# Head attention and feed-forward as one stage over token tiles, in plain fp32, with two norms joined

## The chip, the core and the metric

The kernel runs on one core of one Trainium2 chip. A core has five engines with queues of their own that run side by side: TensorE (matmuls, PE in the profile; its weight loads are PEld), VectorE (DVE), ScalarE (ACT), GpSimd (POOL) and SyncE (SP, which here issues transfers). The metric is the device time of one execution, in microseconds.

## What is computed

A three-part model layer on x of 8 x 64 tokens by 512. First cross attention over a context of 1601 rows. Then the part that is edited, and last a mixture of experts with routing. The edited part, cut from the reference (the outer call applies a norm without gain to x, and the part begins with a norm of its own):

```
x = x + xattn(layernorm(x), ctx)                 # cross attention; its last product is W_O
y = layernorm(x)                                 # no gain, no bias
h = layernorm(y) * ln1_g + ln1_b                 # the second norm in a row
q, k = per-token 32 heads of 16 from h @ Wq.T, h @ Wk.T;  v = h @ Wv.T
att = softmax(nan_to_num(q @ k.T))               # 32 x 32 for each token, heads attend to heads
att2 = att[first half, first half] - lam * att[second half, second half]
o = rmsnorm(att2 @ v) * (1 - 0.8 + 0.6 exp(-0.3))
conn = y + o @ Wo.T + bo
src3 = relu((layernorm(conn) * ln2_g + ln2_b) @ W1.T + b1) @ W2.T + b2     # 512 -> 2048 -> 512
x = x + conn + src3
```

## The kernel before

The 512 tokens are four tiles of 128 (`TT`), tokens on partitions, 512 features along them; a feature-major copy of a tile is four blocks of 128 (`KD`). Stages follow one another, each a block with its own queues and an all-engine barrier behind it: `queries`, `cross_attention`, `head_attention`, `feed_forward`, `route`, `experts`. The order of an engine's work is written out by hand, and semaphores link the engines.

In `head_attention` and `feed_forward` every matmul is done as three (`mm3`, L64 to L66): both operands are split into a high and a low part of type fp32r (ScalarE copies the high part, `high`; GpSimd subtracts to get the low one, `low`, L790), and high x high, high x low, low x high are added. In order: `W_O` is applied to the output of cross attention for all four tiles, x and the bias (added beforehand by GpSimd, L838) are added on VectorE (L997), `normaliser` runs twice over all tiles (`norm1`, `norm2`, L658 to L670), TensorE turns the result, ScalarE applies gain and bias, VectorE splits (L1002, L1004), and 12 projections (three a tile) follow.

The attention of heads has no matmul, since each token has its own 32 x 32 scores. `order` lists products: for each tile `NQ` = 8 pieces "qk" of `QR` = 4 query heads (2048 elements a partition) and `NA` = 4 pieces "av"; the av pieces of a tile come behind the qk pieces of the next. Of three pieces GpSimd multiplies two into the buffers of `prod` (three) and VectorE one into `vprod` (two) (`multiply`, L761 and L765); VectorE reduces all of them (`reduce`, L943). Between them stand `clean` (nan_to_num: L950, L951, and the sum on GpSimd, L807), `row_max` (L955, L957), 32 exponentials a tile on ScalarE with the bias from `nmax` (L906), `row_sum` (L961, and `rlam`, L963), `weights` on GpSimd (L814 to L821), `square`, `mean_square`, `root`, `scale` (L827 to L974). Then TensorE turns the tile (L1077) and applies `Wo`, and `skip` adds it (L984). `low(4)`, for `Wo`, stands in GpSimd's queue among the products of tile 1.

`feed_forward` loads eight more slabs of weights through three buffers, normalises and turns all tiles, and runs 16 steps: `up(f)` makes 128 hidden features for all 512 tokens, ScalarE applies relu (L1177), VectorE and GpSimd split (L1193, L1150), `down(f)` adds to all four tiles.

## Time and profile before

| | us |
|---|---|
| median of 3 runs | 1822.5 (1821.58 to 1823.15) |
| the profiled execution, its own time | 1819.43 |
| its span, first to last instruction | 1817.6 |
| mean granted TensorE clock | 0.887 |
| VectorE busy | 958.4 (53%) |
| TensorE busy | 1425.5 (78%) |
| GpSimd busy | 654.7 (36%) |

How rows are read. A row of the span's slices has 40 digits, one for each 45.4 us: the busy share in tenths, and for PEclk the granted clock in tenths of 2.4 GHz. A row of stretches gives from:to, its length, then for PE, PEld, DVE, ACT and POOL the busy time with the number of instructions, the granted clock, the share of the DMA engines and GB/s. A row of instruction groups gives line, engine, operation, out<-in by name, shape out<-in, count, then busy time in us and mean ns of one, and the idle time before them with what ended it. A row of the timeline gives start, length (of the whole row where it stands for several instructions), engine, line, and in brackets the idle time before it. A plain fp32 matmul has two records.

### The profile page before, as it was taken

What the parts mean: (1) busy time and instruction counts of PE and PEld (TensorE: products, weight loads), DVE (VectorE), ACT (ScalarE), POOL (GpSimd) and SP (SyncE); (2) the same over time, 40 slices, a digit from 0 to 9 for tenths busy, and PEclk for the clock granted to TensorE, in tenths of its full rate; (3) what the DMA queues carried; (4) which work ended last, traced back from release to release, by engine and by line L of the source; (5) the groups of instructions that cost most, each with busy time, mean ns of one, the idle gap of its engine ahead of it and who ended that gap; (6) DMA issues with size and microseconds to landing.
All of it is one profiled execution on the core that took longest, in us unless ns stands there. A gap on an engine that the chain in (4) does not pass through costs nothing. (4 is left out here: it accounts for less than half of the span.)

```text
span 1817.6 us, 23549 instructions
## 1 busy us (share of the span) xinstructions
PE 1425.5 (78%) x8688; PEld 1217.8 (67%) x8688; DVE 958.4 (53%) x2159; ACT 612.2 (34%) x1230; POOL 654.7 (36%) x260
## 2 busy tenths in 40 slices
PE   3599999999999999999996630112389565999995
PEld 2599999999999999999995420001267453555552
DVE  7155545555555555555554598995601553444443
ACT  4144344443445434454434232112321201232231
POOL 4505023050220502205003599895652312344442
PEclk8799999999999999999998765555689686999997
DMA  3401002010020200201003000000500209999999
GB/s 140 167 7 61 25 1 79 7 62 24 1 79 7 79 7 1 80 7 43 1 1 117 35 0 0 0 1 0 191 1 0 99 1 361 336 333 337 342 331 304
DMA packets 42619, 166.70 MB, mean 92 GB/s; under 512 B 5792, under 2 KB 6304, under 8 KB 33952
## 3 DMA queue, kind: packets, MB, share of 16 engines
q1 hardware_dynamic: 32352, 141.32, 21.2%
q0 software_dynamic: 10176, 24.12, 5.3%
q8 instruction: 62, 1.02, 0.2%
q14 instruction: 29, 0.24, 0.0%
HBM read 144.98 MB, written 20.45 MB: 91 GB/s over the span
## 5 line engine op out<-in xcount | busy, mean ns | idle before, releaser
L331 POOL TENSOR_TENSOR c_hi<-craw,ones 128x1608 fp32r<-128x1608 f32 x32 | 91.9, 2871 | 621.8 <-PE ps_x L66 548.1
L64 PE MATMUL ps_x<-wkv_hi,c_hi 128*128 128x256 f32 (+1 forms) x832 | 240.3, 289 | 0.0
L65 PE MATMUL ps_x<-wkv_lo,c_hi 128*128 128x256 f32 (+1 forms) x832 | 233.4, 281 | 0.0
L66 PE MATMUL ps_x<-wkv_hi,c_lo 128*128 128x256 f32 (+1 forms) x832 | 232.8, 280 | 0.0
L64 PE MATMUL ps_x<-c_hi,wkv_hi 128*128 128x402 f32 x512 | 196.2, 383 | 34.0 <-POOL c_lo L334 34.0
L583 DVE TENSOR_TENSOR pT<-ps_x,pT 128x512 fp32r<-128x512 f32 (+1 forms) x224 | 145.6, 651 | 125.9 <-ACT pT L508 122.7
L65 PE MATMUL ps_x<-c_lo,wkv_hi 128*128 128x402 f32 x512 | 178.0, 348 | 0.0
L66 PE MATMUL ps_x<-c_hi,wkv_lo 128*128 128x402 f32 x512 | 177.5, 347 | 0.0
L508 ACT CAST pT<-ps_x 128x512 fp32r<-128x512 f32 (+1 forms) x224 | 124.6, 557 | 140.2 <-PE ps_x L418 136.6
L553 DVE TENSOR_TENSOR vv<-ps_x,vv 128x512 fp32r<-128x512 f32 (+1 forms) x112 | 73.0, 652 | 176.7 <-ACT vv L489 176.7
L64 PEld LDWEIGHTS ps_x<-wkv_hi,c_hi 128*128 128x128 f32 (+1 forms) x832 | 153.2, 184 | 16.9 <-issue 16.9
L489 ACT CAST vv<-ps_x 128x512 fp32r<-128x512 f32 (+1 forms) x112 | 62.3, 556 | 288.1 <-PE ps_x L66 288.1
L1772 PE MATMUL ps_e<-e_w_gu,e_xT 128*128 128x512 f32 x344 | 157.5, 601 | 0.0
L547 DVE SCALAR_TENSOR_TENSOR kT_lo<-ps_x,bk,kT_hi 128x402 fp32r<-128x402 f32 x128 | 81.4, 636 | 140.8 <-ACT kT_hi L483 140.8
L65 PEld LDWEIGHTS ps_x<-wkv_lo,c_hi 128*128 128x128 f32 (+1 forms) x832 | 153.5, 184 | 0.0
L66 PEld LDWEIGHTS ps_x<-wkv_hi,c_lo 128*128 128x128 f32 (+1 forms) x832 | 153.3, 184 | 0.0
L1077 PE MATMUL ps_h<-ident,h_on 128*128 128x128 f32 x16 | 4.4, 432 | 178.8 <-POOL h_on L833 178.8
L433 PE MATMUL ps_x<-pT,vv 128*128 128x256 f32 (+1 forms) x832 | 135.1, 285 | 2.5 <-DVE pT L583 2.5
L566 DVE TENSOR_SCALAR_CACHE_REDUCE prob<-ps_x 128x402 f32<-128x402 f32 (+1 forms) x256 | 131.2, 569 | 0.0
L433 PEld LDWEIGHTS ps_x<-pT,vv 128*128 128x128 f32 (+1 forms) x832 | 124.8, 188 | 5.3 <-DVE pT L583 3.9
L418 PE MATMUL ps_x<-ident,prob 128*128 128x128 f32 (+1 forms) x832 | 127.0, 272 | 0.0
L1077 PEld LDWEIGHTS ps_h<-ident,h_on 128*128 128x128 f32 x16 | 2.9, 217 | 180.8 <-issue 99.0
(290 smaller groups left out, 3232.2 us busy)
## 6 DMA issues: line engine op xcount, KB each, us to landing
e_w_gu<-w_gu SPq DMA_DIRECT2D x49, 1024.0 KB, 8.1
craw<-ctxT SPq DMA_DIRECT2D x32, 804.0 KB, 4.5
e_w_dn<-w_dn SPq DMA_DIRECT2D x48, 512.0 KB, 5.6
f_raw<-slabs SPq DMA_DIRECT2D x8, 1024.0 KB, 4.8
h_raw<-slabs SPq DMA_DIRECT2D x5, 1024.0 KB, 4.9
qbd_dram<-qbd_all SPq DMA_DIRECT2D x2, 2048.0 KB, 6.9
qbd<-qbd_dram SPq DMA_DIRECT2D x16, 256.0 KB, 2.7
wraw<-w_qkv SPq DMA_DIRECT2D x3, 1024.0 KB, 8.4
```

The lines of the kernel that those rows point to most:

```text
L64: nc.tensor.matmul(out, a_hi, b_hi, start=start, stop=False)
L65: nc.tensor.matmul(out, a_hi, b_lo, start=False, stop=False)
L66: return nc.tensor.matmul(out, a_lo, b_hi, start=False, stop=stop)
L331: nc.gpsimd.tensor_tensor(c_hi[:, :, chunk(c)], craw[:, c % 2], ones[:, 0:1].unsqueeze(2).to_broadcast([P, KD, CW]), ALU.mult).then_inc(sp ...
L418: ins = nc.tensor.transpose(ps[0:r, 6 + n % 2, c:c + P], prob[:, 2 * g + j, P * st:P * st + r], ident[:])
L433: ins = nc.tensor.matmul(ps[:, 4 + g, 256 * j:256 * j + 256], vv[0:r, st, 2 * g + j].rearrange("p l c -> p (l c)"), pT[0:r, n % 2, st % 2, ...
L508: nc.scalar.copy(pT[0:r, n % 2, 0:w, :, 0].rearrange("p a j c -> p (a j) c"), ps[0:r, 6 + n % 2, 0:256 * w].rearrange("p (a c) -> p a c", ...
L547: nc.vector.scalar_tensor_tensor(kT_lo[:, m, chunk(c)], ps[:, n % KEY_BANKS, 0:CW], bk[:, 2 * h + m:2 * h + m + 1], f32(kT_hi[:, m, chunk( ...
L553: nc.vector.tensor_tensor(vv[0:r, 2 * v:2 * v + w, :, 1].rearrange("p a j c -> p (a j) c"), ps[0:r, V_BANK[v], 0:256 * w].rearrange("p (a ...
L566: ins = nc.vector.tensor_scalar(prob[:, p, CW * n:CW * n + w], ps[:, 2 * (i % 2) + j, 0:w], 0.0, None, ALU.add, ALU.max, accum_out=pmax[:, ...
L583: nc.vector.tensor_tensor(pT[0:r, n % 2, 0:w, :, 1].rearrange("p a j c -> p (a j) c"), ps[0:r, 6 + n % 2, 0:256 * w].rearrange("p (a c) -> ...
L1772: ins = nc.tensor.matmul(ps[:, GU], xT[:, b, P * g:P * g + P], w_gu[:, b, g], start=(g == 0), stop=(g == KD - 1))
```

## The change

One stage, `head_and_feed_forward`, takes the place of two, and everything from `W_O` on goes tile by tile.

- All 13 weight slabs stay in SBUF as they are (12 buffers; the last slab takes the place of the first). There is no `mm3` in the stage and no high or low part: each matmul is one in plain fp32. Biases come in through a matmul of one row (`ones` by `row`) that opens the sum.
- The two norms in a row use one set of statistics: with v the variance, the second variance is v/(v + eps), and `normed_twice` applies the product of both inverse roots in one pass; `normed_once` gives y. Tiles are normalised in groups 0, 1, and 2 with 3.
- `QR` is 2: twice as many pieces of half the size. The rule of one in three on VectorE stays. `row_max` negates in the reduction, `rlam` moves to ScalarE, z2 is written in place.
- q, k and v have two buffers. Feed-forward of a tile is `up` with 128 columns (tokens) moving, relu on ScalarE, and `down` six steps behind, with eight buffers `fT` (`NF_`); its PSUM is two banks of four pieces each.
- Work of all three kinds is put by hand into the queues, in ScalarE's and TensorE's as below.

```diff
-    NR, NS, NP, NPV = 2, 3, 3, 2
-    QR = 4
+    NP, NPV = 3, 2
+    QR = 2
+    FT, NF_, LAG = FF // P, 8, 6
@@ reductions on VectorE, what stands among them
-                    if t >= 2 and i == 2:
-                        mean_square(t - 2)
-                    if t and i == 4:
-                        row_sum(t - 1)
+                    if t == 0 and i == 3:
+                        attended_in(2)
+                    if t == 0 and i == 5:
+                        attended_in(3)
+                        first_norm(2)
+                    if t == 0 and i == 8:
+                        inverse(2)
...
+                    if t == 0 and i in (10, 12):
+                        normed_twice(2 if i == 10 else 3)
+                        normed_once(2 if i == 10 else 3)
+                    if t >= 2 and i == 3:
+                        mean_square(t - 2)
                     if t >= 2 and i == 5:
                         root(t - 2)
-                    if t >= 2 and i == 7:
-                        attended_low(t - 2)
+                    if t and i == 6:
+                        row_sum(t - 1)
+                    if t >= 3 and i == 9:
+                        second_skip(t - 3)
+                    if t >= 2 and i == 12:
+                        connect(t - 2)
+                        second_norm(t - 2)
+                    if t >= 2 and i == 14:
+                        connection_normed(t - 2)
@@ VectorE behind the last reduction
+            second_skip(TT - 3)
+            connect(TT - 2)
+            second_norm(TT - 2)
             mean_square(TT - 1)
+            connection_normed(TT - 2)
             root(TT - 1)
+            connect(TT - 1)
+            second_norm(TT - 1)
+            second_skip(TT - 2)
+            connection_normed(TT - 1)
+            second_skip(TT - 1)
@@ ScalarE
+            act.wait_ge(c_loaded, 64)
+            std_first(0)
+            turned_h(0)
+            query_key(0)
+            std_first(1)
+            value(0)
+            turned_h(1)
+            query_key(1)
+            value(1)
+            std_first(2)
...
+            turned_c(0)
+            hidden(0, range(0, 4))
+            exponentials(2, range(0, 16))
+            hidden(0, range(4, 8))
+            exponentials(2, range(16, 32))
+            root(1)
+            scaled_sums(2)
+            hidden(0, range(8, 16))
+            value(3)
+            turned_o(1)
+            std_second(1)
+            turned_c(1)
+            hidden(1, range(0, 4))
+            exponentials(3, range(0, 16))
+            hidden(1, range(4, 8))
+            exponentials(3, range(16, 32))
+            scaled_sums(3)
+            root(2)
+            hidden(1, range(8, 16))
...
@@ TensorE
-                    ins = mm3(nc, ps[:, 4 + f % 4], w_hi[s % NS][:, g, c], w_lo[s % NS][:, g, c], a_hi[:, g], a_lo[:, g],
-                              g == 0, g == KD - 1)
+                    ins = nc.tensor.matmul(ps[:, UP + f // 4 % 2, c], slab[:, 5 + 2 * (f // 4), g, c], cT[:, g],
+                                           start=(g == 0), stop=(g == KD - 1))
...
+            attend(0)
+            attend(1)
+            turn_h(0)
+            for w in range(3):
+                project(0, w)
+            attend(2)
+            attend(3)
...
+            turn_h(3)
+            turn_o(0)
+            put_out(0)
+            project(3, 0)
+            project(3, 1)
+            turn_c(0)
+            for f in range(FT + LAG):
+                if f < FT:
+                    up(0, f)
+                if f >= LAG:
+                    down(0, f - LAG)
+            project(3, 2)
+            turn_o(1)
+            put_out(1)
+            turn_c(1)
...
+            for f in range(FT + LAG):
+                if f < FT:
+                    up(2, f)
+                if f >= LAG:
+                    down(2, f - LAG)
+                if f == 9:
+                    turn_o(3)
+                if f == 13:
+                    put_out(3)
+            turn_c(3)
```

The new functions called there: `attend(t)` is bias row and four matmuls with `W_O`; `attended_in(t)` adds x; `first_norm` and `inverse` make the joined norm's factors, with `std_first` on ScalarE between; `turn_h`, `turned_h`, `project`, `query_key`, `value` make q, k, v; `turn_o`, `turned_o`, `put_out` apply `Wo`, and `connect` adds it to y; `second_norm`, `std_second`, `connection_normed`, `turn_c`, `turned_c` make the input of the feed-forward; `second_skip(t)` waits for `down_full` of the whole tile t and adds it to x, to which GpSimd's `skip(t)` has added conn. `hidden(t, fs)` is relu of some of the 16 pieces; a piece needs its batch of four ups, and the `down` eight pieces back for its buffer. `up` waits at every fourth piece for relu of the batch before, and `down(t, f)` for relu of piece f.

## Rows read from the trace of the kernel before

**Rows 1.** The page's slices, 40 of 45.4 us each

```profile
DVE  7155545555555555555554598995601553444443
PEclk8799999999999999999998765555689686999997
```

**Rows 2.** Busy time by stretch, around the edited stages

```profile
976.20:1032.50 56.30, 27.37 (x94) 21.28 (x95) 25.80 (x48) 18.23 (x19) 27.32 (x6) 0.67 0.33 122
1032.50:1258.80 226.30, 40.01 (x151) 30.41 (x149) 195.52 (x101) 60.93 (x278) 200.93 (x55) 0.58 0.00 0
1258.80:1275.60 16.80, 10.43 (x28) 7.50 (x28) 3.80 (x8) 0.80 (x2) 2.09 (x2) 0.67 0.00 0
1275.60:1409.80 134.20, 98.92 (x400) 78.47 (x400) 40.21 (x42) 28.83 (x29) 66.63 (x26) 0.85 0.18 65
1409.80:1523.00 113.20, 60.71 (x265) 50.74 (x266) 59.12 (x159) 12.68 (x15) 24.75 (x13) 0.68 0.32 118
```

**Rows 3.** The timeline at the stage's opening and the first products

```profile
981.14 1.90 ACT L874 CAST h_w_hi<-h_raw 128x2048 fp32r<-128x2048 f32 x1 [2.36 <-DMA h_raw<-slabs]
987.66 0.79 PE L64 MATMUL ps_h<-h_w_hi,h_a_hi 128*128 128x512 f32 x1 [13.37 <-POOL h_w_lo L790]
988.49 3.69 DVE L991 TENSOR_TENSOR h_lprod<-h_lam 128x32 f32<-128x32 f32 x1 [8.78 <-DMA h_lam<-lambdas]
1028.53 1.11 ACT L894 ACTIVATE h_q<-ps_h 128x512 f32<-128x512 f32 x1 [6.43 <-PE ps_h L66]
1032.51 31.55 POOL L761 TENSOR_TENSOR h_prod<-h_q,h_k 128x2048 f32<-128x2048 f32 x6 [13.20 <-ACT h_k L894]
```

**Rows 4.** Groups of instructions by shape, 980 to 1500 us

```profile
L761 POOL TENSOR_TENSOR h_prod<-h_q,h_k 128x2048 f32<-128x2048 f32 x21 | 108.5, 5198 | 13.2 <-ACT h_k L894 13.2
L943 DVE TENSOR_REDUCE h_att<-h_prod 128x128 f32<-128x2048 f32 x21 | 47.7, 2279 | 21.7 <-POOL h_prod L761 21.7
L906 ACT ACTIVATE h_ex<-h_att,h_nmax 128x32 f32<-128x32 f32 x128 | 39.0, 306 | 71.0 <-DVE h_nmax L957 71.0
L807 POOL TENSOR_TENSOR h_att<-h_z 128x1024 f32<-128x1024 f32 x4 | 9.4, 2353 | 7.8 <-DVE h_z L951 7.8
L955 DVE TENSOR_REDUCE h_rmax<-h_att 128x32 f32<-128x1024 f32 x4 | 4.8, 1212 | 2.4 <-POOL h_att L807 2.4
L984 DVE TENSOR_TENSOR oT<-ps_h,oT 128x512 f32<-128x512 f32 x4 | 2.7, 686 | 9.5 <-PE ps_h L66 9.5
L670 DVE TENSOR_SCALAR h_hT<-oT,h_n_mv,h_n_rstd 128x512 f32<-128x512 f32 x4 | 1.9, 541 | 0.0
L814 POOL TENSOR_TENSOR h_w<-h_ex,h_rinv 128x256 f32<-128x256 f32 x4 | 2.5, 618 | 2.9 <-DVE h_rlam L963 2.8
L827 POOL TENSOR_TENSOR h_sq<-h_o 128x512 f32<-128x512 f32 x4 | 6.2, 1554 | 8.3 <-DVE h_o L943 8.3
```

**Rows 5.** Timeline of weight loads: experts' 512-column matmul, cross attention's 128-column one

```profile
1600.37 0.19 PEld L1787 LDWEIGHTS ps_e<-e_w_dn,e_hT 128*128 128x128 f32 x1 [0.24 <-issue]
1600.80 0.19 PEld L1787 LDWEIGHTS ps_e<-e_w_dn,e_hT 128*128 128x128 f32 x1 [0.24 <-issue]
...
805.13 0.53 PEld L403 LDWEIGHTS ps_x<-diag,ones 128*128 128x128 f32 x4
805.57 0.19 PEld L64 LDWEIGHTS ps_x<-c_hi,wkv_hi 128*128 128x128 f32 x1
```

**Rows 6.** Busy time by stretch, in the feed-forward, behind a pause of TensorE

```profile
1323.50:1327.90 4.40, 4.32 (x10) 3.47 (x11) 0.00 (x0) 0.00 (x0) 2.41 (x2) 0.50 0.00 0
1327.90:1345.00 17.10, 17.10 (x74) 13.73 (x73) 1.99 (x3) 3.87 (x4) 7.55 (x4) 0.99 0.01 1
```

**Rows 7.** Timeline: GpSimd's products, and one small VectorE instruction twice

```profile
1070.12 26.33 POOL L761 TENSOR_TENSOR h_prod<-h_q,h_k 128x2048 f32<-128x2048 f32 x5
1092.52 3.96 DVE L963 TENSOR_SCALAR h_rlam<-h_rinv,h_lam 128x16 f32<-128x16 f32 x1
1152.15 0.23 DVE L963 TENSOR_SCALAR h_rlam<-h_rinv,h_lam 128x16 f32<-128x16 f32 x1
```

More of the change, by code:

```diff
@@ new lines, in attend, with turn_h @@
+            def attend(t):
+                out = ps[:, WIDE if t % 2 == 0 else DOWN]
+                if t >= 2:
+                    pe.wait_ge(x1_done, t - 1)
+                nc.tensor.matmul(out, ones[0:1, :], row[0:1, 0], start=True, stop=False)
+                for g in range(KD):
+                    ins = nc.tensor.matmul(out, oT[:, g, P * t:P * t + P], slab[:, W_O, g], start=False, stop=(g == KD - 1))
+                ins.then_inc(x1_full, 1)
+            def turn_h(t):
+                pe.wait_ge(h_done, t + 1)
+                if t:
+                    pe.wait_ge(hT_done, t)
+                for g in range(KD):
+                    ins = nc.tensor.transpose(ps[:, TURN, P * g:P * g + P], h[:, t % 2, P * g:P * g + P], ident[:])
+                ins.then_inc(hT_full, 1)
@@ new lines, in project @@
+            def project(t, w):
+                pe.wait_ge(hT_done, t + 1)
+                pe.wait_ge(w_loaded[W_Q + w], 16)
+                if t:
+                    if w < 2:
+                        pe.wait_ge(qk_done, 2 * (t - 1) + w + 1)
+                    else:
+                        pe.wait_ge(v_done, t)
+                for g in range(KD):
+                    ins = nc.tensor.matmul(ps[:, QKV + w], hT[:, t % 2, g], slab[:, W_Q + w, g], start=(g == 0), stop=(g == KD - 1))
+                ins.then_inc(qkv_full, 1)
@@ new lines, in turn_o, with put_out @@
+            def turn_o(t):
+                pe.wait_ge(on_done, t + 1)
+                if t == 0:
+                    pe.wait_ge(hT_done, TT)
+                else:
+                    pe.wait_ge(cT_done, t)
+                    pe.wait_ge(onT_done, t)
+                for g in range(KD):
+                    ins = nc.tensor.transpose(ps[:, TURN, P * g:P * g + P], on[:, P * g:P * g + P], ident[:])
+                ins.then_inc(onT_full, 1)
+            def put_out(t):
+                pe.wait_ge(onT_done, t + 1)
+                pe.wait_ge(w_loaded[W_OUT], 16)
+                if t == 0:
+                    pe.wait_ge(x1_done, TT)
+                else:
+                    pe.wait_ge(conn_done, t)
+                nc.tensor.matmul(ps[:, WIDE], ones[0:1, :], row[0:1, 1], start=True, stop=False)
+                for g in range(KD):
+                    ins = nc.tensor.matmul(ps[:, WIDE], onT[:, g], slab[:, W_OUT, g], start=False, stop=(g == KD - 1))
+                ins.then_inc(src_full, 1)
@@ L1232, in _, with down @@
-            for f in range(FT + 2):
-                if f < FT:
-                    up(f)
-                if f >= 2:
-                    down(f - 2)
+            def down(t, f):
+                n = FT * t + f
+                if f == 0:
+                    if t == 0:
+                        pe.wait_ge(x1_done, TT)
+                    else:
+                        pe.wait_ge(x2_done, t)
+                    nc.tensor.matmul(ps[:, DOWN], ones[0:1, :], row[0:1, 2], start=True, stop=False)
+                if t == 0 and f % 4 == 0:
+                    pe.wait_ge(w_loaded[6 + 2 * (f // 4)], 16)
+                pe.wait_ge(f_done, n + 1)
+                nc.tensor.matmul(ps[:, DOWN], fT[:, n % NF_], slab[:, (6 + 2 * (f // 4)) % LATE, f % 4], start=False, stop=(f == FT - 1)
+                                 ).then_inc(down_full, 1)
```

632 lines of the change are left out of this document (307 added, 325 removed).

## The prediction

> **What bounds the kernel now.** I read the share of the span first [rows 1], then the busy time of each engine in stretches around the edited code [rows 2], then the order of time at its two ends [rows 3], and last the groups of instructions by shape for prices [rows 4]. The first thing to see is that the edited stage is one piece of the span with nothing beside it: it opens behind an all-engine barrier at 976.2 us and its last vector add ends at 1409.8 us, 433.6 us out of 1817.6. Route and experts follow behind barriers and are untouched, as is cross attention, so every microsecond taken from the stage comes off the end, and nothing else can give or take. Inside it there are four stretches with different limits. From 976.2 to 1032.5 is a serial opening (56.3 us): load, split weights, project, two norms one after the other, turn, project. From 1032.5 to 1258.8 VectorE and GpSimd are the bound, 195.5 and 200.9 us busy of 226.3, and TensorE works 40 us of it, mostly the tail of the projections. From 1258.8 to 1275.6 (16.8 us) the last tile's output projection is waited for. From 1275.6 to 1409.8 (134.2 us) the feed-forward runs alone, TensorE 98.9 us busy, the others mostly idle. TensorE idle in one long stretch and vector engines idle in the next: that is what a pipeline over tiles can use [rows 2].
>
> **Prices of a plain fp32 matmul.** No matmul of this stage is plain fp32 today, but the experts have 512-column ones: each is two records, and two weight loads of the stream start 0.43 us apart (1600.37, 1600.80), so one matmul costs 0.86 us at full clock [rows 5]. A 128-column one (ones by diag) is two records too, and four records take 0.44 us (805.13 to 805.57): 0.22 us each [rows 5]. A split product's single matmul of 512 columns takes 17.1 / 74 = 0.231 us in the warm stretch of the feed-forward [rows 6], so the three of `mm3` cost 0.69 us. Dropping the splits therefore raises TensorE's time by a quarter (0.86 against 0.69). The Trainium skill speaks against the change here too: "FP8 and Floating Point Precision", section TensorE Precision Notes, says that true FP32 takes 4 passes through the array, against three for the split; by that rule the ratio would be 4/3 where the rows give 1.24, so the trace agrees in direction and the rows' figure is smaller.
>
> **The opening.** Removed: the copies to high parts, the GpSimd low parts and with them the wait until 987.66; the second pass of norm statistics; the splits of the turned tile; and the opening now needs tile 0 only. New path: slab 0 has landed at 981.1 (ScalarE starts on it at 981.14, TensorE only at 987.66 [rows 3]). TensorE is at half clock then, a matmul costs 2 x 0.86; five per tile (bias row and four), at half clock for 5 to 6 us (4.4 in [rows 6]; here it has stood still longer), so tile 0 is ready at about 988.3 and tile 1 at 992.6. Tile 0's add and joined norm take about 2.5 us on VectorE, to 990.8; but ScalarE first waits for all four small loads, queued behind 4 MB now. In the profile the lambdas behind 3.5 MB were there at 988.5 [rows 3]; half a MB more and two more loads put that at about 992. Then root, inverse, one normalising pass (0.54 us, [rows 4]) to 993.3, four transposes and four evictions to 995.2, two projections of 4 x 0.86 us and the eviction of q and k (1.1 us each, [rows 3]) to 1003.6. The first product starts there and not at 1032.5: **28.9 us saved**. The other tiles' start-up work goes beside the products; inverse of tiles 2 and 3 waits on ScalarE, which comes to it only behind both projected tiles at about 1027, some 4 us after VectorE: I count 2 us, since GpSimd fills its three buffers meanwhile.
>
> **The loop of products.** QR goes from 4 to 2: 96 products of 1024 elements for 48 of 2048, still one in three on VectorE. Two engines share something: GpSimd's run of five products takes 26.33 us and the small VectorE instruction issued beside it at 1092.52 takes 3.96 us, until GpSimd's product ends at 1096.45, where a like one takes 0.2 us alone [rows 7]; a reduction keeps its 2.28 us beside GpSimd [rows 4]. So I add up, over the loop, GpSimd's time and that of VectorE's two-input and scalar instructions, and leave the reductions out. (The Trainium skill, "SBUF — State Buffer", section Who interferes with whom, calls it an exclusive lock that is held for the whole instruction and never taken by `tensor_reduce`. By that rule the two times add up as well, and the trace agrees.) Before: 32 products x 4.45 us free of waits (an estimate: 26.33 less two VectorE products of about 2.3, over 5, and less a little), `low(4)` 4.5, per tile the sum 2.3 and three weights of 0.6 to 0.7, 17.6 in all, squares and scales 6.3 (six of about 1.0 free of waits, 1.55 with them [rows 4]), and on VectorE 16 x 2.3 + 7.6: 214.7 us against 226.3 measured, so 11.6 us did not overlap. After: 64 products x 2.28 (half of 4.45 and some 0.05; a 1024-element add takes 2.35, [rows 4]) = 146, sums, weights, squares, scales 23.9, two skips 2.5, no `low(4)`; VectorE 32 x 1.2 + 5.2 + normalising passes and small ones 5.6 = 49.2. Sum 221.6; with smaller pieces I take 9.4 us of lost overlap instead of 11.6: 231 us, **4.7 us dearer**. VectorE's own list stays below it: 96 reductions at 1.14 (1.21 alone, [rows 4]) 109, products 54 with waits, the new norm work about 20, less the fused negation and the scaled sums moved to ScalarE (about 15).
>
> **The waits that the pipeline adds.** VectorE's queue holds `second_skip(0)` behind the tenth product of tile 3, and behind it stand all later reductions, for which GpSimd's three buffers wait. It needs all of feed-forward tile 0. ScalarE's order lets `hidden(0, 8..16)` run only behind `root(1)` and `scaled_sums(2)`, that is, behind VectorE's `row_sum(2)` at the seventh product of tile 3. By then TensorE has come to down(8), which waits for it; behind it are one up and eight downs in all: 4 x 0.22 + 8 x 0.86 = 7.8 us at full clock, about 10.8 because it stood still before and starts at half clock [rows 6]. VectorE arrives three products (6 us) after `row_sum(2)`: a wait of 4.8 us. `connect(1)` then needs project(3, 2) 3.4, turn and two ScalarE copies 2.1, put_out 4.3 after that, against an add and three products, 6 us: 3.8 us more. Of these 8.6 I count **7 us** lost, since GpSimd runs ahead by its three buffers. Exponentials (9.8 us a tile, 32 x 0.306, [rows 4]) are beside the products as before. The loop: 231 + 2 + 7 = 240 us, so its last reduction is at 1003.6 + 240 = 1243.6, not at 1258.8.
>
> **The tail.** Feed-forward of tiles 0 and 1 has gone beside the products; tiles 2 and 3 have not. What is left of tile 1 behind `root(2)` (10.8 us) and put_out(2) (6) is shorter than the products of av(3) (19), so nothing of it is waited for. Then two adds, statistics, mean_square(3), normalise (add 0.68, pass 0.54, [rows 4]), turn, evict: 5.5 us. Tile 2 on TensorE: 64 x 0.22 + 17 x 0.86 = 28.7 us, plus turn_o(3) and put_out(3) inside it 4.8, plus 2.8 for a start at half clock: 36.3. Then `second_skip(2)` stands ahead of `connection_normed(3)`: 3.5 us until tile 3 is turned. Tile 3: 28.7 + 2.5 for the clock. Last add and clearing of the semaphores 2.6. Together 79.1: the next stage starts at 1322.7 in place of 1410.0.
>
> **Sum.** -28.9 (opening) + 13.7 (loop 240 for 226.3) - 72.1 (16.8 + 134.4 after the loop, now 79.1) = -87.3 us. The profiled execution took 1819.4 us by its own time (span 1817.6), so the changed one should take 1732.1; the median of the timed runs lies 3.1 us above that profiled execution, so I forecast **1735 us**.
>
> **Rivals.** (a) *Half clock in the first two feed-forward tiles.* TensorE stands still in each of them, waiting for ScalarE. At 1.2 GHz tile 0 ends at about 1187, project and put_out bring tile 1's start to 1210, it takes 57 us, put_out(2) ends at 1279 and not before the last reduction: the tail starts 35 us later, **1770 us**. For it: the granted clock was 0.50 for 4.4 us behind a pause. Against: it was 0.99 right after [rows 6]. (b) *The half-size pieces overlap better.* A wait for the other engine's instruction is half as long; if lost overlap falls from 11.6 to 3 us and all stalls to 4, the loop takes 229: **1724 us**. For it: the wait of 3.96 us is that of a whole 2048-element product [rows 7]. Against: the reductions are no shorter in sum. (c) *Slower: TensorE at half clock is the bound of the stage.* Four times 57.4 us from the start of feed-forward tile 0 at 1133, project 7, three put_outs 26, and the hand-overs (turn, evict, norm, 5 us each) 20 are 282: the stage ends at 1416, 6 us later than today, **1828 us**. Each microsecond at full clock gives one back, so it is slower than before only if all but some 6 us of that stretch stay at 1.2 GHz. Against it: 17.1 us of unbroken matmuls at 0.99 [rows 6], and in tiles 2 and 3 fT holds eight pieces, so nothing interrupts TensorE for long. By the Trainium skill, "TensorE: Matmul & The Clock Gate", section HAM oscillation, a stream with recurring pauses drops back to the slow clock each time; that would be (a) in the first two tiles, and [rows 6] shows both levels, not which one the new loop gets.
>
> **How the numbers follow.** Forecast 0.57, (a) 0.18, (b) 0.22, (c) 0.03. Around the forecast, lost overlap (3 to 18 us), the stalls (3 to 15) and the half-clock starts (0 to 6) reach some 10 us down and 15 up: 1725 to 1750 by itself. The range takes in (b) with some of that, and (a): 1714 to 1772; left out are (c) and the outer ends of the others. This kernel can be told from no change at about 0.2%: faster 0.96, same 0.01, slower 0.03.
>
> **What would show it.** First product at 1004 us; 96 reductions at about 1.2 us each; a VectorE wait for TensorE's last `down` of tile 0 in tile 3's products, about 5 us; the last reduction near 1244; granted clock 1.0 in both last feed-forward tiles and 29 us each; the next stage at 1323. Wrong if the first product waits for loads, if GpSimd's half-size product takes clearly more than 2.3 us, or if a 128-column plain matmul doesn't stream at 0.22 us with 128-column weights loaded for each.

## The result

The changed kernel takes **1744.1 us** (median of 4 runs, 1742.1 to 1745.7) against 1822.0 us before (4 runs, 1821.1 to 1823.2): a ratio of 0.957, 95% interval 0.956 to 0.959, or 78 us less. The forecast was 1735 us, range 1714 to 1772. The profiled execution took 1745.7 us (span 1743.8), where the sum had given 1732.1: it is 13.6 us above the sum.

TensorE's slices of before first (VectorE's are in [rows 1]), then the page of after, its share of busy time and its slices:

```profile
PE   3599999999999999999996630112389565999995
```

```profile
PE 1475.6 (85%) x8888; PEld 1213.9 (70%) x8888; DVE 912.6 (52%) x2185; ACT 600.7 (34%) x1297; POOL 559.6 (32%) x263
...
PE   3499999999999999999999762276795668999994
...
DVE  6145455555555555555555399885702733444442
...
PEclk9699999999999999999999886587897677999997
```

A slice is 43.6 us. VectorE's full slices (9988, the 24th to 27th, with the 5 and 7 behind them) now have TensorE at 2 to 7 tenths (622767). Before, the two took turns: VectorE's 9899 (the same places, of 45.4 us each) stand beside TensorE's 3011. The same in stretches cut where the work changes: opening, products, tail, route and experts (to set beside [rows 2]; columns are the length, busy us of each engine, granted clock, DMA share, GB/s):

```profile
977.30:1005.40 28.10, 21.30 (x44) 8.68 (x45) 5.49 (x17) 7.66 (x13) 0.04 (x1) 0.81 0.94 376
1005.40:1253.40 248.00, 134.21 (x484) 75.93 (x482) 207.13 (x191) 77.08 (x338) 197.31 (x88) 0.76 0.04 17
1253.40:1332.10 78.70, 68.19 (x346) 46.80 (x346) 7.61 (x19) 13.11 (x44) 4.57 (x4) 0.93 0.00 1
1332.10:1743.80 411.70, 331.74 (x1200) 196.32 (x1200) 185.71 (x717) 90.42 (x185) 137.07 (x99) 0.87 0.81 270
```

| stretch | before | predicted | after |
|---|---|---|---|
| stage opens | 976.2 | 976.2 | 977.3 |
| opening, to the first product | 56.3 | 27.4 | 28.1 |
| products, to the last reduction | 226.3 | 240 | 248.0 |
| behind the last reduction | 151.2 | 79.1 | 78.7 |
| route, experts, output | 407.5 | 407.5 | 411.7 |

("Before", the stretch behind the last reduction is the 16.8 us and 134.4 us of the prediction.) So opening and tail came as worked out, to 1 us. The miss is 8 us in the products, 4.2 us in code that the change does not touch, and 1.1 us by which the stage opens later. The opening and the first steps of the products, on VectorE, ScalarE and GpSimd of after (to set beside [rows 3]):

```profile
991.97 0.21 DVE L1070 TENSOR_SCALAR h_var<-h_mv,h_rvar 128x1 f32<-128x1 f32 x1
992.26 1.28 ACT L892 ACT_TABLE_LOAD   x1 [12.43 <-DVE h_var L1070]
993.56 0.21 ACT L892 ACTIVATE h_std<-h_var 128x2 f32<-128x2 f32 x1
...
1005.08 0.20 ACT L892 ACTIVATE h_std<-h_var 128x2 f32<-128x2 f32 x1
1005.34 0.17 DVE L1076 RECIPROCAL h_rstd<-h_std 128x2 f32<-128x2 f32 x1 [7.96 <-ACT h_std L892]
1005.36 2.34 POOL L780 TENSOR_TENSOR h_prod<-h_q,h_k 128x1024 f32<-128x1024 f32 x1 [147.76 <-ACT h_k L908]
1005.54 2.18 DVE L1078 TENSOR_TENSOR h_rboth<-h_rstd 128x1 f32<-128x1 f32 x1
1007.75 2.52 DVE L1084 TENSOR_SCALAR h_h<-x_tok,h_mv,h_rboth 128x512 f32<-128x512 f32 x1
1010.19 2.56 DVE L1088 TENSOR_SCALAR h_y<-x_tok,h_mv,h_rstd 128x512 f32<-128x512 f32 x1
1012.67 0.18 DVE L1164 TENSOR_TENSOR h_lprod<-h_lam 128x32 f32<-128x32 f32 x1
...
1012.99 2.33 DVE L1044 TENSOR_REDUCE h_att<-h_prod 128x64 f32<-128x1024 f32 x2
```

This is a step that the prediction had not seen. ScalarE's queue has the root of tile 1's norm (L892 at 1005.08) behind the evictions of q and k of tile 0, so VectorE waits 7.96 us for it, and then three of its instructions run beside GpSimd's first products. The multiplication of one element a partition takes 2.18 us, until 1007.72; the product beside it ends at 1007.70. The first reduction starts 7.6 us after the first product.

The other end of it, tile 3's products: VectorE's two waits for TensorE, and what TensorE had waited for (the forecast had 4.8 and 3.8 us):

```profile
1194.61 0.69 DVE L1151 TENSOR_TENSOR x_tok<-ps_h,x_tok 128x512 f32<-128x512 f32 x1 [6.43 <-PE ps_h L1309]
1204.27 0.69 DVE L1130 TENSOR_TENSOR h_y<-ps_h,h_y 128x512 f32<-128x512 f32 x1 [4.33 <-PE ps_h L1273]
```
```profile
1183.55 2.04 PE L1309 MATMUL ps_h<-h_slab,h_fT 128*128 128x512 f32 x2 [15.02 <-ACT h_fT L964]
```
```profile
1198.88 2.33 POOL L780 TENSOR_TENSOR h_prod<-h_q,h_k 128x1024 f32<-128x1024 f32 x1 [5.15 <-DVE h_att L1044]
```

VectorE waits 6.43 us for the last down of tile 0 and 4.33 us for put_out(1). TensorE began those downs only at 1183.55, since the hidden pieces had been queued on ScalarE behind root(1) and the scaled sums. The last row is how the stall reaches GpSimd: its three buffers are full and it waits 5.15 us for a reduction.

### The profile page after: what moved, and what is told of

Read it like the earlier page. It is cut to its first block and busy times, and to the rows that moved or that the text cites. A ratio compares the mean times of both kernels' runs of the same rounds, so it can differ in the third digit from the quotient of the medians.

```text
span 1743.8 us, 24185 instructions
## 1 busy us (share of the span) xinstructions
PE 1475.6 (85%) x8888; PEld 1213.9 (70%) x8888; DVE 912.6 (52%) x2185; ACT 600.7 (34%) x1297; POOL 559.6 (32%) x263
## 5 line engine op out<-in xcount | busy, mean ns | idle before, releaser
L780 POOL TENSOR_TENSOR h_prod<-h_q,h_k 128x1024 f32<-128x1024 f32 x44 | 115.5, 2655 | 159.7 <-ACT h_k L908 147.8
L64 PEld LDWEIGHTS ps_x<-c_hi,wkv_hi 128*128 128x128 f32 x512 | 97.6, 191 | 34.6 <-POOL c_lo L334 34.5
```

The costliest lines, as they stand in the source:

```text
L64: nc.tensor.matmul(out, a_hi, b_hi, start=start, stop=False)
L780: return eng.tensor_tensor(buffer.rearrange("p (a b d) -> p a b d", a=QR, b=2 * H2), q[:, t % 2, r].unsqueeze(2).to_broadcast(shape), k[:, ...
```

## The experiments

Each time is a median of 5 runs (4 in experiment 3, 6 in experiment 5, 12 in experiment 8), and each ratio is to the kernel before run beside it. A difference of two ratios is given in us of 1822; subtracting the medians instead gives figures up to 3 us apart from these, and the intervals are 2 to 7 us wide on each side. So for differences of a few us the profiles' own marks decide: the start of the last reduction and the start of the last add of the stage. The stage itself opens between 975.6 and 977.3 us in these profiles, whatever the edit, so a mark can move by up to 1.7 us without it. The length of the products, from the first product to the end of the last reduction, is free of this:

| kernel | products, us | against |
|---|---|---|
| before | 226.4 | |
| before with half pieces (8) | 231.6 | before, +5.2 |
| changed | 248.0 | |
| root early (1) | 245.5 | changed, -2.5 |
| hidden pieces early (2) | 239.7 | changed, -8.4 |
| no feed-forward beside the products (3) | 237.0 | changed, -11.0 |
| both orders (4) | 236.8 | changed, -11.2 |
| passes moved (5) | 238.4 | both orders, +1.6 |
| two of five (6) | 245.8 | both orders, +8.9 |
| one of four (7) | 244.5 | both orders, +7.7 |
| half of the ups (11) | 236.5 | both orders, -0.3 |
| fastest (10) | 239.8 | |
| add on VectorE (12) | 246.7 | fastest, +6.9 |

**1. The root ahead of q and k.**

```diff
-            query_key(0)
             std_first(1)
+            query_key(0)
```

> Edit: ScalarE takes the root of tile 1's first norm ahead of the eviction of q and k of tile 0, not behind it. Theory A (order of ScalarE): the opening of the product loop lost time because VectorE had to wait 7.96 us for that root, and then ran its small instructions of tile 1 (2.18, 2.52 and 2.56 us each) against GpSimd's first products, so that its first reduction began at 1012.99 us and not near 1007.7. With the root early the wait is gone, the first reduction begins near 1007.5, and the kernel takes 4 to 6 us less: about 1739 us. Theory B (sum of the two engines): the products of GpSimd and VectorE share something and their sum is what the loop takes, the first reduction only moves within it; GpSimd stood still 1.8 us there, so the gain is 0 to 2 us: 1742 to 1744.

Measured: 1739.1 us, ratio 0.9555 (0.9541 to 0.9568), 2.9 us less than the changed kernel. The first reduction starts at 1007.51 and not at 1012.99, 5.5 us earlier, but the last one only 2.8 us earlier (1249.4 for 1252.2). The wait was real, and half of it was paid in the end: GpSimd had been filling buffers meanwhile. It lies between the two theories; this order costs 2.5 to 2.8 us by the profiles. (The intervals of the two ratios overlap, so the timed runs alone would not settle it.)

**2. The hidden pieces ahead of the root.**

```diff
+            hidden(0, range(8, 16))
             root(1)
             scaled_sums(2)
-            hidden(0, range(8, 16))
```

> Edit: ScalarE runs the second half of the hidden pieces of feed-forward tile 0 ahead of root(1) and scaled_sums(2), not behind them. Theory A (the pipeline's wait is paid by the loop): TensorE no longer stands 15.0 us at down(8); the wait of second_skip(0) of 6.43 us is gone and connect(1), 4.33 us, with it or nearly; the kernel takes 6 to 10 us less, 1734 to 1738. Theory B (GpSimd is the bound and runs ahead by three buffers while VectorE waits): VectorE's waits show elsewhere, for GpSimd's products; the kernel takes at most 2 us less. Theory C (the wait moves): the hidden pieces now hold root(1) back and row_sum(2) or the scaled sums come late, 0 to 3 us gained.

Measured: 1737.2 us, ratio 0.9528 (0.9515 to 0.9542), 7.8 us less. Both waits are gone from VectorE's rows: second_skip(0) runs at 1187.86 and connect(1) at 1193.41, without a bracket. The last reduction starts at 1243.6, **8.6 us** earlier. So 8.6 of the 10.8 us of VectorE's waits were paid by the loop: theory A. (The prediction had put 8.6 us of waits and 7 of them paid.) But the last add of the stage is only 5.2 us earlier. The other 3.3 us went back in the tail, 2.7 of them at one place, the first ups of tile 3. TensorE's rows there, first in after and then in this kernel, each followed by a row of its stretch with the granted clock (1.00 and 0.55):

```profile
1298.36 0.66 PE L1280 MATMUL ps_h<-ident,h_cn 128*128 128x128 f32 x4 [1.51 <-DVE h_cn L1146]
1300.61 6.52 PE L1294 MATMUL ps_h<-h_cT,h_slab 128*128 128x128 f32 x56 [1.59 <-ACT h_cT L953]
```
```profile
1300.60:1306.00 5.40, 5.39 (x48) 5.39 (x49) 0.00 (x0) 1.14 (x4) 0.00 (x0) 1.00 0.01 3
```
```profile
1292.67 9.21 PE L1294 MATMUL ps_h<-h_cT,h_slab 128*128 128x128 f32 x56 [1.60 <-ACT h_cT L953]
```
```profile
1292.60:1299.00 6.40, 6.33 (x32) 6.33 (x33) 0.00 (x0) 0.02 (x1) 0.00 (x0) 0.55 0.01 3
```

The same 56 matmul records, behind the same pause of 3.76 us between the last down of tile 2 and the first up of tile 3 (1.51 us idle while the tile is normalised, 0.66 us of turning, 1.59 us idle while it is evicted; the recorded text of experiment 9 calls it 3.65 us): 6.52 us at 1.00 in one kernel, 9.21 us at 0.55 in the other, that is, at 2.4 GHz and mostly at 1.2.

**3. Nothing of the feed-forward beside the products.**

```diff
+            for t in range(TT):
+                turn_c(t)
+                for f in range(FT + LAG):
+                    ...
```

> Edit: the feed-forward of all four tiles runs behind the attention loop, nothing of it beside the products; all else (plain fp32, joined norm, early first product) stays. Theory A (the loop hides two tiles of feed-forward at the price of its waits only): the loop loses its waits for second_skip(0) and connect(1), 6.43 and 4.33 us, so its last reduction comes 8 to 11 us earlier, and the tail grows by two tiles of about 29.3 us and two hand-overs of 3.5 us, 65.6 us: 55 us slower, 1799 us. Theory B (TensorE and ScalarE beside the products slow the two vector engines): the products get faster too, the loop gains 20 us or more and the kernel is at most 45 us slower, under 1789.

Measured: 1803.6 us, ratio 0.9897 (0.9882 to 0.9912), 59.4 us more than the changed kernel. Last reduction at 1241.1, 11.0 us earlier, last add at 1388.2, 57.9 us later. Theory A: beside the products, two tiles of feed-forward cost the vector engines their waits (8.6 of the 11.0 us by experiment 2) and next to nothing else. For the other 2.4 us, this edit also takes `second_skip(0)` (0.69 us) and two `connection_normed` (0.15 and 0.55 us each) out of the products, 2.1 us of VectorE's own work. It also splits the gain: of the 78 us, 59 come from hiding two tiles, and 19 from everything else together. By this kernel's marks the second part (20 us there) is 27 us of shorter opening and 4 us behind the last reduction, less 10.6 us by which its products are longer than before. What plain fp32, the joined norm and the one-tile opening are worth apart was not measured.

**4. Both orders.** Experiments 1 and 2 together.

> Edit: the two ScalarE orders together (root of tile 1's first norm ahead of q and k of tile 0; second half of the hidden pieces of feed-forward tile 0 ahead of root(1) and scaled_sums(2)). They sit 180 us apart and share no buffer. Theory A (independent): the gains in the loop add, 2.8 + 8.6 us by the last reductions of the two profiles, last reduction at about 1240.8 us; with a tail of 79 to 82 us the kernel takes 1732 to 1735 us. Theory B (the pair's sum caps the loop): the second gain eats the first, the last reduction stays at 1243 and the kernel at 1737 us.

Measured: 1734.9 us, ratio 0.9512 (0.9484 to 0.9539), last reduction at 1240.3, 11.9 us earlier; expected were 11.4. The two are independent. The products now run from 1004.7 to 1241.5.

**5. Normalising passes out of tile 0's products** (on top of 4).

```diff
-                    if t == 0 and i in (10, 12):
-                        normed_twice(2 if i == 10 else 3)
-                        normed_once(2 if i == 10 else 3)
+                    if t == 0 and i == 10:
+                        normed_twice(2)
...
                     reduce(at_av[t - 1, i])
+                    if t == 1 and i == 0:
+                        normed_once(2)
+                        normed_twice(3)
+                        normed_once(3)
```

> Edit: as the one with both ScalarE orders, and three of the four normalising passes of tiles 2 and 3 (x to h, x to y) leave VectorE's queue in tile 0's products for the place where VectorE waits for GpSimd's first av product of tile 0. Theory A (the first tile's products are bound by VectorE's own list, which has no idle time there, not by the sum of both engines): the section loses 3 to 4 us, the wait of 3.3 us takes the passes in, and the kernel is 2 to 4 us faster than with both orders alone. Theory B (what counts is the sum of both engines, as the prediction added it up): the passes cost the same in either place, 0 to 0.5 us.

Measured: 1735.5 us, ratio 0.9526 (0.9489 to 0.9562), no difference that these runs can tell; last reduction 2.0 us *later* than in 4 (1.6 us by the length of the products). Tile 0's products end 0.8 us earlier by the clips that follow them (1046.5 for 1047.3), not 3 to 4. Theory A falls. Two of the passes are long in 4 (1.64 and 2.55 us, where the other two take 0.54), because they wait for GpSimd's products, and that wait goes to what comes next: VectorE's product behind the removed pass takes 3.34 us (at 1036.07) where in 4 it took 1.21 us (at 1038.08).

**6 and 7. Another share** (on top of 4), two products of five on VectorE, then one of four, in place of one of three.

```diff
-        by_vector = [n for n in range(len(order)) if n % 3 == 2]
+        by_vector = [n for n in range(len(order)) if n % 5 in (2, 4)]
```

> Edit: as the one with both ScalarE orders, and two of five products on VectorE in place of one of three (58 on GpSimd and 38 on VectorE for 64 and 32). A VectorE product takes 1.22 us when GpSimd is idle and 2.2 us beside it, a GpSimd one 2.33 us. Theory A (the loop is bound by the sum of the two engines' two-input instructions): six products cost 1.2 us each less of it, 4 to 7 us faster than with both orders alone. Theory B (VectorE's list is the bound nearly everywhere): six more products on it at 1.2 to 2.2 us each, 7 to 13 us slower.

> Edit: as the one with both ScalarE orders, and one of four products on VectorE in place of one of three (72 on GpSimd, 24 on VectorE for 64 and 32). Two of five made the loop about 9 us longer. Theory A (VectorE's list is the bound nearly everywhere): eight products fewer on it at 1.2 to 2.2 us, 5 to 12 us faster. Theory B (one in three is near the balance of the two, so either way costs): GpSimd's list grows by 8 x 2.33 = 18.6 us, and the loop by 5 to 15 us.

Measured: two of five 1744.3 us (0.9554, 0.9529 to 0.9579), last reduction 8.4 us later than in 4; one of four 1739.9 us (0.9540, 0.9514 to 0.9566), 7.7 us later. Both ways cost, so one of three is the best of the three shares. In the first case the loss came although the sum of both engines' products falls at the prices of products that wait for nothing (1.21 and 2.31 us each: 180 us for 187; with their waits it is 231 for 230). In the second it came although VectorE's own products fell from 61 to 47 us.

**8. Only the smaller pieces, in the kernel before** (the places of the other steps among them doubled).

```diff
-    QR = 4
+    QR = 2
```

> Edit: the kernel before with its products cut in halves (QR = 2, 96 products of 1024 elements), the places of the other steps doubled; nothing else of the change. Theory A (the prediction's price): each half-size product costs GpSimd 0.05 us more (+3.2 us), against 2.2 us of better overlap, and the reductions are off the bound: 0 to 5 us slower than before, 1822 to 1827. Theory B (rival b): lost overlap falls by 8 us and more, 5 to 9 us faster, 1813 to 1817.

Measured: 1829.8 us, ratio 1.0029 (1.0010 to 1.0048), **5.3 us slower**, and its products take 5.2 us longer (231.6 for 226.4). The prediction's sum gives this part alone about +3.0: 3.6 on GpSimd (146 for 142.4) and 1.6 on VectorE (38.4 for 36.8), less 2.2 of lost overlap. Its groups, and behind them the group of whole "av" pieces in the kernel before (that of whole "qk" pieces is in [rows 4]):

```profile
L761 POOL TENSOR_TENSOR h_prod<-h_q,h_k 128x1024 f32<-128x1024 f32 x44 | 119.6, 2748 | 16.8 <-ACT h_k L894 12.7 <-DVE h_att L943 2.9 <-DVE h_o L943 1.2
L765 POOL TENSOR_TENSOR h_prod<-h_att,h_v 128x1024 f32<-128x1024 f32 x20 | 50.7, 2567 | 0.1
```
```profile
L765 POOL TENSOR_TENSOR h_prod<-h_att,h_v 128x2048 f32<-128x2048 f32 x11 | 59.3, 5406 | 0.6
```

With their waits GpSimd's 64 half products take 170.3 us, its 32 whole ones 167.8. Without waits the shortest half product takes 2.31 us and the shortest whole one 4.45, so halves are dearer by 0.08 us each where the sum had 0.05. On VectorE the shortest take 1.21 and 2.22 us. Rival (b) of the prediction is refuted by this, for the kernel before. In the changed kernel it has no run: with whole pieces its buffers do not fit in SBUF beside the twelve slabs (4096 bytes a partition are wanted for `h_o` where 224 are left).

**9. The pause in the tail** (on top of 4). TensorE turns tile 3 between the last downs of tile 2.

```diff
+                if f == 18:
+                    turn_c(3)
-            turn_c(3)
...
-            second_skip(TT - 2)
             connection_normed(TT - 1)
+            second_skip(TT - 2)
```

> Edit: as the one with both ScalarE orders; TensorE turns tile 3's normalised tile between the last downs of tile 2 (behind down(2, 12)) and VectorE makes it ahead of second_skip(2), so that TensorE has no pause of 3.65 us between the last two feed-forward tiles. Theory A (the pause and, in part, what the clock takes behind it): the pause is gone, last add 3.0 us earlier, and where the clock had fallen behind the pause (6.4 us at 0.55 in one profile, none in two) up to 2.9 us more: 3 to 5 us faster than with both orders alone. Theory B (the tail is bound elsewhere: hidden pieces from ScalarE, or the add of the last tile): 0 to 1 us.

Measured: 1730.3 us, ratio 0.9481 (0.9454 to 0.9508), 5.6 us less than 4; last add at 1315.4 for 1318.8, 3.4 us earlier. The profile of 4 had kept the full clock behind the pause, so 3.4 us is the pause alone (3.76 us in 4, 0.27 here). The timed runs gave more, but the difference is within their intervals.

**10. The fastest** (on top of 9).

```diff
+                    if t == TT and i == 6:
+                        connect(TT - 2)
+                        second_norm(TT - 2)
+                        connection_normed(TT - 2)
...
+            nc.scalar.activation(rlam[:, 0:1], keep["ones"][:, 0:1], ACT.Sqrt)
             act.wait_ge(c_loaded, 64)
```

> Edit: as the one with the tail closed, and two more: VectorE takes connect(2), the norm behind it and the normalised tile ahead of the last product of tile 3 and of second_skip(1) and mean_square(3), 2.7 us earlier by the profile; and ScalarE loads the table of the root during the weight load, which stood on the way to the first product with 1.28 us. Theory A (both are on the path that ends last): 2.7 + 1.3 = 4 us faster than with the tail closed. Theory B (the loop's later steps or the clock take them back): 0 to 2 us.

Measured: **1724.4 us**, ratio 0.9454 (0.9426 to 0.9481), 4.9 us less than 9; last add at 1310.35, 5.05 us earlier. Of these 5.05 us, 0.9 are a stage that happens to open earlier (ScalarE's first row at 975.81 for 976.74). Feed-forward of tile 2 runs from 1242.96 on and not from 1248.29. The table load of 1.28 us off the path gave only 0.6 us: from the opening to the first product it is 27.46 us for 28.07, because the small loads now end ScalarE's wait:

```profile
991.47 0.21 ACT L892 ACTIVATE h_std<-h_var 128x2 f32<-128x2 f32 x1 [11.59 <-DMA h_b<-b]
```

By the ratios this kernel is 21 us under the changed one, and it computes the same.

**11. Half of the ups' contraction left out** (on top of 4; the first feed-forward product sums over 256 of 512 rows).

```diff
-                for g in range(KD):
+                for g in range(KD // 2):
```

> Edit: as the one with both ScalarE orders, and the first product of the feed-forward contracts only 256 of its 512 rows (half of the 128-column plain fp32 matmuls left out), so the output is not the reference's. Theory A (TensorE binds the two last tiles and is hidden in the two first): 2 tiles x 32 matmuls x 0.22 us = 14.1 us, and about 1.5 us more where these run at half clock; 14 to 16 us faster than with both orders alone, the last reduction where it was. Theory B (hand-overs and ScalarE's evictions bind the tail): 5 to 8 us. Theory C (TensorE's time counts in the first tiles too): over 18 us, and the last reduction earlier.

Measured: 1718.4 us, ratio 0.9416 (0.9390 to 0.9441), 17.5 us less; last reduction where it was (1240.0 for 1240.3), last add 11.7 us earlier. TensorE's time in tiles 0 and 1 is free, in tiles 2 and 3 it counts in full. That the profile shows 11.7 and not 14.1 us is mostly the clock again: behind the pause of tile 3 it was 0.52 here, and 28 records took 6.16 us where 56 had taken 6.52, so that about 2.9 us were lost there (an estimate: 6.16 less half of 6.52). The other four runs took 1717.0 to 1718.5 us, the profiled one 1723.4.

```profile
1281.70:1287.80 6.10, 6.04 (x28) 5.97 (x28) 0.00 (x0) 1.15 (x5) 0.00 (x0) 0.52 0.00 0
```

**12. The add of the clipped scores on VectorE** (on top of 10).

```diff
+                dve.wait_ge(z_done, 2 * t + 2)
+                nc.vector.tensor_tensor(x, z1[:], x, ALU.add).then_inc(zsum_done, 1)
...
-                if t < TT:
-                    add_z(t)
```

> Edit: as the fastest so far (both ScalarE orders, closed tail, earlier connect(2), earlier table load), and the add of the two clipped parts of the scores (1024 elements, once a tile) is done by VectorE right behind the clips, not by GpSimd between products. Theory A (at the borders between tiles the loop pays the hand-over from VectorE to GpSimd and back): a GpSimd add takes 2.3 us, 3.3 us beside VectorE's product, and VectorE stands 2.45 us once and about 3.3 us in each later tile before it goes on; the same add costs VectorE 1.2 us. 1.2 us in tile 0 and 1 to 2.5 us in each of three more: 4 to 9 us faster. Theory B (VectorE's list is as full as GpSimd's, as the two other shares of the products showed): 4 x 1.2 us more on VectorE against 4 x 3.0 less on GpSimd, the wait only moves to its next product: within 2 us.

Measured: 1733.4 us, ratio 0.9518 (0.9502 to 0.9533), 11.7 us **slower**: neither theory. By the profiles 6.6 us of these are in the stage (last reduction and last add both 6.6 us later), and 2.5 us behind it, in code that is the same; the rest is between the profiled runs and the medians. The products are longer though GpSimd has 12 us less to do. VectorE's groups in the products (1002 to 1250 us), of the fastest kernel first (the clip to the upper bound, then the reductions that wait for GpSimd), then of this one (the same two, and the add):

```profile
L1098 DVE TENSOR_SCALAR h_att<-h_att 128x1024 f32<-128x1024 f32 x4 | 2.7, 684 | 0.0
L1045 DVE TENSOR_REDUCE h_o<-h_prod 128x64 f32<-128x1024 f32 x20 | 23.9, 1213 | 13.6 <-POOL h_prod L784 13.6
```
```profile
L1096 DVE TENSOR_SCALAR h_att<-h_att 128x1024 f32<-128x1024 f32 x4 | 11.2, 2809 | 0.0
L1043 DVE TENSOR_REDUCE h_o<-h_prod 128x64 f32<-128x1024 f32 x20 | 23.9, 1210 | 3.8 <-POOL h_prod L784 3.8
L1098 DVE TENSOR_TENSOR h_att<-h_z,h_att 128x1024 f32<-128x1024 f32 x4 | 6.9, 1725 | 0.1
```

VectorE's waits did shrink, as theory A had it: 9.8 us less for the av products and 2.5 us less for the add. But its own list grew by 18.8 us. The adds are 6.9 of them. The clips are 10.5: the one shown takes 2.81 us for 0.68 in each of the four tiles, and the one before it 5.2 us in sum for 3.2. In the fastest kernel GpSimd's queue holds the add, which waits for the clips, so that no product runs beside the second of them. Without the add GpSimd goes on with its products, and the clip stands beside one. Normalising passes account for another 5.2 us (`h_y` 5.1 for 3.1, `h_cn` 4.8 for 1.6). VectorE's own products cost 3.8 us *less* in sum (57.5 for 61.3). Together 18.8 less 12.3 is 6.5 us, the size of what the marks show.

Where the two engines meet also changes the price of a product from place to place. GpSimd's rows in tile 1's products, first of the fastest kernel, then of this one, and behind them VectorE's in the same order:

```profile
1049.51 30.13 POOL L780 TENSOR_TENSOR h_prod<-h_q,h_k 128x1024 f32<-128x1024 f32 x11
```
```profile
1069.90 5.64 POOL L780 TENSOR_TENSOR h_prod<-h_q,h_k 128x1024 f32<-128x1024 f32 x2 [0.26 <-DVE h_att L1043]
```
```profile
1069.71 2.16 DVE L780 TENSOR_TENSOR h_vprod<-h_q,h_k 128x1024 f32<-128x1024 f32 x1
...
1075.29 2.17 DVE L780 TENSOR_TENSOR h_vprod<-h_q,h_k 128x1024 f32<-128x1024 f32 x1
```
```profile
1070.87 2.46 DVE L780 TENSOR_TENSOR h_vprod<-h_q,h_k 128x1024 f32<-128x1024 f32 x1
...
1076.74 2.45 DVE L780 TENSOR_TENSOR h_vprod<-h_q,h_k 128x1024 f32<-128x1024 f32 x1
```

In the fastest kernel GpSimd runs 11 products without a wait, and VectorE's period of three pieces is 5.6 us (1069.71 to 1075.29). In this one GpSimd's buffers are full. It waits for a reduction before every second product and then starts just ahead of VectorE's product, which takes 2.45 us for 2.16: the period is 5.9 us (1070.87 to 1076.74). This costs 0.3 us a period here, but it is not what made the kernel slower, since over all 32 of VectorE's products the time fell.

## Why the prediction was right, point by point

**The opening**, -28.9: it came to -28.2 us (56.3 to 28.1). The sum's single terms held: slab 0 first, half clock, joined norm, two projections. That the whole came so near is in part luck, since two errors nearly cancel. The table load of 1.28 us (992.26) was not in the sum. Against it, the sum had ScalarE wait 1.2 us for the small loads; the last of them landed at 991.9, ahead of VectorE's variance at 992.18, so it did not wait. Experiment 10 shows that this wait was the next one: with the table load gone, the loads end it. The opening of the stage itself lies 1.1 us later than in the profile of before, ahead of any changed code.

**The pieces.** The prediction's "4.7 us dearer" is the whole loop after against before, with `low(4)` gone and skips and norms added; half pieces alone are about +3.0 in it. They cost 5.3 us, 5.2 by the length of the products (experiment 8). The terms before add up to 215.2 us and not 214.7, which leaves 11.1 us of lost overlap and not 11.6; this changes nothing else, since the 9.4 us after were chosen and not worked out.

**The pipeline's waits**, 4.8 and 3.8 us, 7 of them paid: 6.43 and 4.33 us, 8.6 paid (experiment 2). Mechanism, place and cause were right; the size was low by 1.6 us.

**The loop**, 240: 248.0. This is the term that was mis-sized. 1.6 us are the waits; 2.8 us are the root of tile 1's norm in ScalarE's queue (experiment 1), which the prediction did not follow through that queue though it did so for the hidden pieces; the products free of both take 236.8 us (experiment 4), 3.8 above the 231 + 2. Some 2.2 of these 3.8 us fit the half pieces, 5.2 us for the 3.0 in the sum (experiment 8): in the changed kernel too no product of GpSimd takes less than 2.31 us, half of them 2.34 or more, where the sum had 2.28. The rest stays open. Experiment 5 showed that moving three normalising passes out of tile 0's products takes none of it back. The basis of the sum, GpSimd's time and VectorE's two-input time added and the reductions left out, is itself only half right: by it, experiments 6 and 12 had to gain, and both lost. What VectorE loses depends on which of its instructions stand beside GpSimd's (experiments 5 and 12), and the 9.4 us of lost overlap took that in as one number. That the sum came out near with it was shown for this order and this share only.

**The lock between the two engines** held as told: 2.18 us for one element beside a product that ends at the same moment. The Trainium skill, "SBUF — State Buffer", section Who interferes with whom, adds that issue order decides who blocks. By that rule the price of a VectorE product depends on which engine started first, and the trace agrees, in the kernel of experiment 12: VectorE's product takes 1.21 us at 1054.50, where GpSimd's begins behind it (1054.66) and takes 3.24 us, and 2.44 us at 1059.13, where GpSimd's are under way.

**The tail**, 79.1: 78.7, and 68.2 of it TensorE at 0.93. In its parts: to the first up of tile 2 6.6 us (5.5 in the sum), tile 2 36.9 (36.3), the pause 3.8 (3.5), tile 3 29.5 (31.2), the end 1.9 (2.6). The parts that were too small and those that were too large nearly cancel. Ups at 0.22 us and downs at 0.86 us, as priced from [rows 5], and experiment 11 confirmed that they count there in full. Plain fp32 being a quarter dearer than the split product was affordable because half of it is hidden. The half clock was taken at one start (6.1 us at 0.61). Behind the pause of 3.76 us the clock stayed full, and the 2.5 us that the sum had for it there were not needed.

**Behind the stage**, 0: +4.2 us, which the prediction did not allow for. It is not of the change. The code there is the same in all kernels, and from its first row to the end of the span it takes 407.5 to 413.0 us over the fourteen profiles: 407.5 in the kernel before, which is the lowest of all, 412.1 in the kernel before with half pieces (experiment 8), and 408.0 and 413.0 in those of experiments 1 and 2. Loads fill this part (DMA share 0.81). The first difference to be seen, 1.3 us, is already in its first wait, ScalarE's for a weight slab. What sets the rest is not known.

**The rivals.** (a), half clock in the first two feed-forward tiles: did not come. The clock was 0.88 in 1130 to 1165 us and 0.89 in 1200 to 1245, and experiment 11 moved no reduction. (b), better overlap of half pieces: refuted by experiment 8, in the kernel before. (c), TensorE as bound: refuted by experiment 11 for the loop.

**Sum.** +1.1 (stage opens later), -28.2, +21.7 (248.0 for 226.3), -72.5 (78.7 for 151.2), +4.2: -73.7 us, from a span of 1817.6 to 1743.8.

## What to carry to other kernels

In a pipeline over tiles, write down for each in-order queue what stands ahead of the one step that another engine waits for. Here two moves of a step in ScalarE's queue gave 10.7 us (7 of which the prediction had counted as lost), and a third, on TensorE and VectorE, 3.4 us more by the profiles. Where two engines contend, try the share one step to each side: neither the sum nor the longer list told which way it should go. And before work is taken off one of them, look at what it was waiting for: the engine that waits may be what leaves the other one alone. Here taking 12 us off GpSimd made the products 6.6 us longer.

## What the runs showed of the hardware that was not expected

**One pause, two clocks.** Eight profiles have the same pause of 3.76 us between the last two feed-forward tiles. In the changed kernel and those of experiments 1, 4, 5 and 7, the 56 records behind it took 6.52 us (granted clock 1.00). They took 8.15 us in experiment 6 (0.73) and 9.21 us (0.55) in experiment 2, and in experiment 11 half of them took 6.16 us (0.52). Behind the longer pause ahead of tile 2, 9.5 to 11.2 us in the same kernels, the records were slower every time (8.1 to 9.4 us for the 56, and granted clock 0.50 in experiment 11); behind the three pauses of 2.0 us in experiment 3 they took 6.52 us each time. The Trainium skill, "TensorE: Matmul & The Clock Gate", section HAM oscillation, has a stream with recurring pauses fall back at each of them; behind the pause of 3.76 us the trace agrees in three of eight, and the fall cost up to 2.9 us. What decides between the two is not known. So this pause is a risk and not a price, and it is cheaper to fill it (experiment 9).

**Less work on GpSimd, later end.** A clip of 128x1024 on VectorE takes 0.68 us while GpSimd waits and 2.81 us beside GpSimd's products, in all four tiles (experiment 12). It has one tensor to read, as has the normalising pass, 0.54 us alone and 2.56 us beside a product: not only products of two tensors are held up. The reductions keep their 1.21 us in both kernels.
